# Row statistics of the later batches in two holes of VectorE's list, and pieces of weights split from round 0 on

## The reference, cut to what matters

```
B, T, D = 16, 256, 256;  HEADS = 16
h = layernorm(x)                                  # per token
shift, scale, gate = split(silu(time) @ mod_w + mod_b, 3)
h = h * (scale + 1) + shift
q, k, v = split(h @ w_qkv, 3), by heads
q = rope(layernorm(q) * q_norm_w); k = rope(layernorm(k) * k_norm_w)
attn = softmax(q k^T / sqrt(16));  out = x + (attn v) @ w_out * gate
```

## Time and profile before

| | us |
|---|---|
| median of 3 runs | 1384.66 (1384.63 to 1385.9) |
| the profiled execution, its own time | 1386.06 |
| its span | 1384.2 |
| TensorE matmul busy | 1227.4 (89%) |
| VectorE busy | 883.5 (64%) |
| ScalarE busy | 633.3 (46%) |
| GpSimd busy | 330.5 (24%) |

### The profile page before, as it was taken

One profiled execution on the slowest core, in us unless ns is written; L12 is line 12 of the kernel. 1 busy time (PEld: TensorE's weight loads), 2 busy tenths in 40 slices (PEclk: granted clock), 3 DMA queues, 4 the chain that ended last, 5 costly groups with the idle time before them and its releaser, 6 DMA issues.

```text
span 1384.2 us, 34408 instructions
## 1 busy us (share of the span) xinstructions
PE 1227.4 (89%) x14232; PEld 982.0 (71%) x14232; DVE 883.5 (64%) x2091; ACT 633.3 (46%) x1191; POOL 330.5 (24%) x311
## 2 busy tenths in 40 slices
PE   4489999999997878159899999999999999999996
PEld 2347676767664333049899999999988888888884
DVE  4978787878773499856565565656555555555552
ACT  2267777777775799413233333333323333333331
POOL 2554545454442399600000000000000000000000
PEclk9689999999999899659999999999999999999996
DMA  9212121212123000057888888888810000000000
GB/s 340 91 47 93 47 94 47 93 47 94 47 93 123 1 0 1 15 243 296 324 354 338 335 327 345 358 345 339 337 75 10 18 18 10 18 10 18 10 18 18
DMA packets 37898, 188.29 MB, mean 136 GB/s; under 512 B 3056, under 2 KB 13424, under 8 KB 29040
## 3 DMA queue, kind: packets, MB, share of 16 engines
q1 hardware_dynamic: 37744, 186.10, 35.1%
HBM read 160.66 MB, written 25.17 MB: 134 GB/s over the span
## 4 chain that ended last, share of the span: by engine, by line
PE 48%; DMA 4%; issue 3%; DVE 2%; ACT 0%; SPq 0%; POOLq 0%; POOL 0%; ACTq 0%
PE pr L1387 6%; PE py L1291 4%; DMA w<-weight_halves 4%; PE ph L1275 4%; PE ph L1276 4%; PE ph L1277 4%; PE py L1293 4%; PE py L1292 4%; PE pys L1426 4%; PE pys L1430 4%; PE phs L1413 2%; PE phs L1409 2%; PE phs L1411 2%; PE pys L1428 2%; PE pr L1398 2%
## 5 line engine op out<-in xcount | busy, mean ns | idle before, releaser
L1114 ACT ACTIVATE g<-ph,b 128x256 f32<-128x256 f32 x256 | 121.5, 475 | 273.5 <-PE ph L1277 273.5
L549 DVE TENSOR_REDUCE mx<-pR 128x4 f32<-128x1024 f32 x128 | 156.3, 1224 | 66.0 <-PE pR L707 64.5
L1222 DVE CAST ghi<-g 128x256 fp32r<-128x256 f32 x256 | 74.7, 292 | 154.0 <-ACT g L1114 153.8
L1493 DVE STREAM_TRANSPOSE preT<-pr 128x64 f32<-128x64 f32 x256 | 63.8, 249 | 163.4 <-PE pr L1387 163.0
L1291 PE MATMUL py<-ghi,w 128*128 128x256 f32 x512 | 147.6, 288 | 18.3 <-issue 16.9
L1275 PE MATMUL ph<-xhi,w 128*128 128x256 f32 x512 | 146.3, 286 | 17.3 <-DMA w<-weight_halves 17.3
L1468 ACT ACTIVATE hs<-preT 128x32 f32<-128x32 f32 x256 | 58.7, 229 | 199.6 <-DVE preT L1493 198.1
L1276 PE MATMUL ph<-xlo,w 128*128 128x256 f32 x512 | 145.9, 285 | 0.0
L1277 PE MATMUL ph<-xhi,w 128*128 128x256 f32 x512 | 145.8, 285 | 0.0
L1292 PE MATMUL py<-glo,w 128*128 128x256 f32 x512 | 145.3, 284 | 0.0
L1293 PE MATMUL py<-ghi,w 128*128 128x256 f32 x512 | 145.2, 284 | 0.0
(11 more groups left out here) (195 smaller groups left out, 2981.0 us busy)
## 6 DMA issues: line engine op xcount, KB each, us to landing
w<-weight_halves SPq DMA_DIRECT2D x66, 2048.0 KB, 12.0
weight_halves<-wparts SPq DMA_DIRECT2D x40, 512.0 KB, 4.1
modw<-in_ew SPq DMA_DIRECT2D x32, 256.0 KB, 4.6
xn<-in_x_tok SPq DMA_DIRECT2D x4, 1024.0 KB, 11.8
XT<-in_x_dm SPq DMA_DIRECT2D x2, 2048.0 KB, 14.2
out_dm<-staged SPq DMA_DIRECT2D x16, 256.0 KB, 2.0
modw<-in_sw SPq DMA_DIRECT2D x8, 256.0 KB, 4.3
modw<-in_mod_w SPq DMA_DIRECT2D x1, 768.0 KB, 7.1
```

What stands on the lines that cost most here:

```text
L549: nc.vector.reduce_max(mx[:, :, 2 * j:2 * j + 2].rearrange("p t s -> p s t"), pR[k][:].rearrange("p s (t k) -> p s t k", t=TC), AX.X).then ...
L1114: nc.scalar.activation(g[:, t % RING], ph[t % RING][:, 0:T], ACT.Gelu_apprx_tanh, bias=b1[:, n, f:f + 1]).then_inc(gelu_done, 1)
```

## The change

Two things move. The statistics of batches 4 to 11 are computed in one pass in round -3 behind normalise(1), and those of 12 to 15 at the start of round -2; the three passes at the end of round -3 are gone. normalise(1) is written out ahead of the first pass and keeps its place among the other steps. Second, pieces are no longer split, stored and followed by a load in rounds -3 to -1; rounds 0 to 5 take three each and rounds 6 to 16 two each, 40 in all. Pieces 0 and 1 are loaded ahead of the rounds as before.

```diff
+        def pieces_to(r):
+            return max(0, 2 * (r + 1) + min(r + 1, 6))
...
 # SyncE, one(r, par)
-                for n in range(2 * (r + 3), 2 * (r + 4)):
+                for n in range(pieces_to(r - 1), pieces_to(r)):
                     store_piece(sp, n)
                     if n + 2 < PIECES:
                         load_piece(sp, n + 2)
...
 # GpSimd, one(r, par)
-                for n in range(2 * (r + 3), 2 * (r + 4)):
+                for n in range(pieces_to(r - 1), pieces_to(r)):
                     split_piece(pool, n)
                 if has(r, 3):
                     rotate(r + 3)
...
 # VectorE, one(r, par)
+                if r == -3:
+                    normalise(1)
+                    dve.wait_ge(x_in[1], 16)
+                    dve.wait_ge(x_in[2], 16)
+                    token_norms(4, 12)
+                if r == -2:
+                    dve.wait_ge(x_in[3], 16)
+                    token_norms(12, 16)
...
-                if has(r, 4):
+                if r > -3 and has(r, 4):
                     normalise(r + 4)
...
                 if has(r, 3):
                     scale_qk(r + 3)
-                if r == -3:
-                    for q in range(1, 4):
-                        dve.wait_ge(x_in[q], 16)
-                        token_norms(4 * q, 4 * q + 4)
```

More of the change, by code:

```diff
@@ L234, in split_piece @@
                 .then_inc(pieces_split, 1)
+        def pieces_to(r):
+            return max(0, 2 * (r + 1) + min(r + 1, 6))
+        assert pieces_to(B) == PIECES
         qk_groups = qkraw[:].rearrange("p t (g e) -> p (t g) e", e=HD)
```

## The result

The median of nine runs is 1374.68 us (1369.56 to 1380.14), beside 1388.27 us for nine runs of the kernel before (1384.63 to 1390.73). The ratio is 0.9912 with a 95% interval of 0.9891 to 0.9932: faster by 0.9%, 9.4 to 15.1 us on 1388.27. The forecast was 17.4 us and 1367.3 us. The direction held, and so did the largest term; the clock term did not, and 1374.68 lies over the range. Of the 7.4 us between it and the forecast, 3.6 are the base, which rose from 1384.66 to 1388.27 with six more runs, and 3.8 are the gain, 13.6 us by the medians. The spread of both kernels is much wider than the three runs shown with the kernel before (1.3 us) had suggested.

What follows compares the result with a forecast made beforehand. The prediction took VectorE's list to set the pace in the opening stage, delaying the first score matmul. Terms: 14.0 + 3.7 - 0.3 = 17.4 us, so 1384.66 - 17.4 = 1367.3 us; range 1364.8 to 1373.5.

Steps and rivals of the forecast that it cites:

- the clock in round -1: TensorE in round -1: idle time gone, clock rises near 48 us and stays up, saving 3.7 us.
- Statistics in the first hole: VectorE, waiting from 21.00 us: one pass over 8 batches takes 9.4 us; batch 0 becomes 0.4 to 0.5 us later.
- Pieces out of rounds -3 to -1: GpSimd: rotate(0) starts 3.2 us earlier, at 34.25; removing the splits of rounds -2 and -1 gives nothing more.
- The last pass beside rotate(0): VectorE, round -2: token_norms(12, 16) from 34.25 takes 9.7 us, ending near 43.9; sums_of_squares(1) can start at 44.6.
- the two bounds alone: VectorE, round -2: the last pass costs between 6.05 us undisturbed and 11.50 us beside splits and rotation.
- The loss that the prediction estimated: Rotation in round -2: three steps each wait some 0.2 us for VectorE, making 14.0 into 13.4; not charged.
- 14.0 us up to the first score matmul: TensorE's first score matmul moves from 62.99 to 49.0 us, winning 14.0; 12.6 with the long pass.
- the clock as it was: Rival, round -1: clock stays at the lower level, gain without 3.7 us, 1371.0 us or 1372.4 with long pass; 24%.
- The third piece: GpSimd, rounds 0 to 5: third split delays the rotation, mostly absorbed by ScalarE's idling; costs 0.3 us, bounds 0 to 2.
- the 3%: Rival, slower than before: third load's landing in rounds 0 to 5 from 8.9 us on makes it over 0.2% slower; 3%.

Runs made afterwards that it cites:

- norms_only: The kernel after with the statistics moved as in the change but the pieces left as in the kernel before; ratio to the kernel before 0.9923.
- filled: The kernel after with 18 additional matmuls of 128x256 in round -1 where TensorE waits, their results unread; ratio to the kernel before 0.9875.
- fill_wide: The kernel after with additional unread matmuls where TensorE waits, 10 in round -1 and 17 in round -2; ratio to the kernel before 0.9887.
- before_again: The kernel before, without an edit, for a second trace and as a control; ratio to the kernel before 1.0002.

## Why the prediction was wrong, by its own steps

The step that failed is the clock in round -1, priced at 3.7 us; a second miss is the base of three runs.

- **Statistics in the first hole.** Right: 9.2 us instead of 9.4, the sums of batch 0 0.4 us late, x already there.
- **Pieces out of rounds -3 to -1.** Right for rotate(0): 34.40 us, 34.3 forecast. Wrong in that removing the splits of rounds -2 and -1 gives nothing more: beside them a pass took 7.06 us instead of 6.05 in the kernel before, and normalise(2) 1.94 instead of 0.73 in norms_only.
- **The last pass beside rotate(0).** Right: it ended at 43.75 us, 43.9 forecast, and the sums of batch 1 started at 44.44, 44.6 forecast. The walk through the times of both engines paid; the two bounds alone (6.05 and 11.50) would have left 5 us open. The rotation took 39.67 - 34.40 = 5.27 us. The loss that the prediction estimated for it by the rule in the Trainium skill, SBUF — State Buffer, "Who interferes with whom", did not appear.
- **14.0 us up to the first score matmul.** Right: 14.3 by the start times of the two traces, 14.5 by the lead, which is 30.1 to 31.2 us in the five traces with both halves of the change and no added work.
- **The clock in round -1, 3.7 us.** This is the step that failed. Its size was about right: 3.67 us between two executions of the kernel before, and from 23.1 (the mean of the five) to 19.8 with added work. Its assignment was wrong twice. The trace of before showed one draw of something that varies between executions, and I took it for a property of the kernel; and taking away the idle time ahead of the score matmuls was not enough, since a wait of 2.07 us within round -1 was left, behind which the level fell to 0.50 from 53.6 to 63.9 us, with qk_raw at 6.38 us in it. That this one wait made it fall is not shown by itself, as the filled kernels shorten or fill all the waits of the round together. The change did not win 3.7 there: in the traces to hand it averages 23.1 us after and 21.7 before (two draws), a loss of about 1.4 if these few count. The Trainium skill, TensorE: Matmul & The Clock Gate, Part 1, says that activity releases the throttle; fill_wide, where the level stayed up, agrees. My use of it against the rival, that a level once released stays through the short waits of round -1, went beyond that sentence, and the runs contradict it. That rival, the clock as it was, had 24% and a gain of 13.7 us, beside 13.6 measured by the medians.
- **The third piece, 0.3 us.** The place and the queue were right, the size a little small: 0.1, 1.1 and 0.5 us in the three traces of the kernel after, inside the 0 to 2 that I had allowed. The waits were longer than forecast: GpSimd's for modw was 7.1 to 9.2 us in the first trace of after, not 5 to 7, and high_parts' up to 1.04 us, not 0.5. The ground for the 3%, that no row has a landing over 8.4 us, holds for the rounds only: the loads of pieces 0 and 1, issued at 15.7 and 16.4 us in the kernel before, landed after 17.7 and 17.6 us.
- **The sum.** 14.4 - 1.4 - 0.6 (the mean of the three) = 12.4 us, beside 12.2 us of 1388.27 by the ratio. That they meet so closely is in part luck, as the stages behind round 5 are left out and each term is a mean of a few traces that differ by more.
- **The range.** It rested on three runs within 1.3 us. The kernel before spreads over 1382.35 to 1394.24 us in all its runs, and its median against 1384.66 rose to 1388.27 with six more; on the old base a gain of 13.6 us would have given 1371.1, inside the range. The traces of one and the same beginning differ by up to 3.7 us in round -1, 3.7 in the expert stage, and, from the last routed matmul to the end of the span, 378.2 to 380.1 between three traces of after.

The experts stage of after, 3.0 us longer than before's, is not of the change as far as the traces tell: the kernels that have both halves show 396.1 to 400.0 us there, the two traces of before 397.0 and 397.7, and the other traces with a changed beginning lie on both sides. The granted clock does not explain it: 0.99 in this stage in both. TensorE was busy as long (376.7 us before, 376.1 after), so what grew is its idle time; its waits for VectorE's glo were 0.5 us before and 4.5 after, but 6.6 in before_again. The cause stays open.

## What to carry to other kernels

Lay the two engines' new times side by side before pricing moved work; here that gave six milestones within 0.4 us. A gain that hangs on TensorE's clock is only the change's own if a second trace of the kernel before shows the same level at the same place; otherwise hold the level with work of TensorE's own, in amounts that fit the waits. A transfer that is issued and awaited within one round puts its landing time in front of whatever stands behind the wait, so put the step that others wait for ahead of it.

## What the runs showed of the hardware

- With the same program and the same idle time before it, the clock in round -1 rose at 78.0 us in one execution and at 67.8 in another.
- A wait of 2.07 us amid matmul work was followed by a fall to 0.50 in after (2.05 and 2.23 us in its two repeats, with the same fall). The four kernels with added work in the waits of round -1 ran that round at 1.00.
- Small matmuls added at waits can be free, if they fit: fill_wide has 10 more of them in round -1 and 17 in round -2, and its round -1 took 19.8 us, the same as the fastest execution without them. filled has 18 in round -1, the same clock of 1.00, and took 21.3 us.
- With four splits in GpSimd's list VectorE's three passes took 24.6 us, without them 21.7; all of the 2.9 us is in the 13 small instructions, which ran beside a rotation or a split, and the statistics and aggregation kept their 2.7 and 0.64 us. Beside GpSimd's work one small instruction of 0.17 us took up to 2.26.
